# A recurrence's TensorE loop that covers all 64 blocks, entered at the first chunk and closed at the last

## The reference, cut to what matters

```python
def _step(Sm, inputs):
    q_t, k_t, v_t, beta_t = inputs
    Sk = jnp.einsum('bhde,bhe->bhd', Sm, k_t)
    delta = v_t - Sk
    Sm = Sm + beta_t[..., None] * jnp.einsum('bhd,bhe->bhde', delta, k_t)
    o_t = jnp.einsum('bhde,bhe->bhd', Sm, q_t)
    return (Sm, o_t)
...
outputs, then:  outputs @ wo + bo
```

## Time and profile before

| | us |
|---|---|
| median of 3 runs | 3170.09 (3166.7 to 3174.82) |
| the profiled execution's time | 3168.27 |
| its span in the trace | 3166.5 |
| TensorE busy | 3037.5 (96%) |
| VectorE busy | 1941.0 (61%) |
| ScalarE busy | 1420.6 (45%) |
| GpSimd busy | 1222.5 (39%) |
| chain that ended last, share of TensorE | 83% |

### The profile page before, as it was taken

The page is one execution under the profiler, slowest core; times in us unless marked ns, Lnnn a source line. Parts: engine busy times, 40 slices in busy tenths (PEclk is TensorE's granted clock), DMA queues, the critical chain, the costliest instruction groups (busy, mean ns, idle before and its releaser), DMA issues.

```text
span 3166.5 us, 148606 instructions
## 1 busy us (share of the span) xinstructions
PE 3037.5 (96%) x67876; PEld 2488.1 (79%) x67876; DVE 1941.0 (61%) x3190; ACT 1420.6 (45%) x3226; POOL 1222.5 (39%) x1225
## 2 busy tenths in 40 slices
PE   5999999999968999999999999999999999999998
PEld 4777777777757999999888787877778787777876
DVE  5888878878758999998513443444444344444434
ACT  5554545444413555555454433444443344444334
POOL 1446565655635877766311221112222112122211
PEclk8999999999978999999999999999999999999999
DMA  3545555554575777777661232222222222222220
GB/s 105 161 141 179 156 161 160 153 163 141 161 224 170 225 227 229 230 217 215 200 201 57 68 79 67 58 76 77 57 70 77 67 58 76 77 58 73 73 67 27
DMA packets 471354, 402.34 MB, mean 127 GB/s; under 512 B 68032, under 2 KB 391744, under 8 KB 471104
## 3 DMA queue, kind: packets, MB, share of 16 engines
q1 hardware_dynamic: 460960, 382.39, 41.5%
q10 hardware_dynamic: 10144, 16.63, 1.8%
HBM read 199.69 MB, written 153.09 MB: 111 GB/s over the span
## 4 chain that ended last, share of the span: by engine, by line
PE 83%; DVE 7%; issue 4%; SPq 3%; DMA 2%; ACT 1%; POOL 0%; DVEq 0%; ACTq 0%
PE bank L238 18%; PE bank L240 17%; PE bank L239 17%; PE bank L1280 14%; PE bank L1365 6%; SPq L1697 3%; PE bank L477 3%; PE bank L429 2%; DMA x2T<-HT 1%; PE bank L438 1%; PE bank L1769 1%; PE bank L421 1%; PE bank L1758 1%; PE bank L412 1%; DVE tmp L1527 1%
## 5 line engine op out<-in xcount | busy, mean ns | idle before, releaser
L2015 DVE TENSOR_TENSOR glo<-gl,gh 128x512 fp32r<-128x512 f32 x256 | 202.0, 789 | 702.5 <-ACT gh L1887 701.0
L1883 ACT ACTIVATE gl<-bank,b1m 128x512 f32<-128x512 f32 x256 | 176.3, 689 | 693.7 <-PE bank L240 693.7
L238 PE MATMUL bank<-h,w_hi 128*128 128x512 f32 x1024 | 404.8, 395 | 0.1
L240 PE MATMUL bank<-h,w_lo 128*128 128x512 f32 x1024 | 400.4, 391 | 0.0
L240 PE MATMUL bank<-w_hi,glo 128*128 128x512 f32 x1024 | 399.6, 390 | 0.0
L238 PE MATMUL bank<-w_hi,gh 128*128 128x512 f32 x1024 | 399.3, 390 | 0.0
L239 PE MATMUL bank<-h,w_hi 128*128 128x512 f32 x1024 | 398.8, 389 | 0.0
L239 PE MATMUL bank<-w_lo,gh 128*128 128x512 f32 x1024 | 398.3, 389 | 0.0
L1280 PE MATMUL bank<-ringA 32*32 32x32 f32 x16384 | 344.0, 197 | 12.9 <-issue 8.1
L1280 PEld LDWEIGHTS bank<-ringA 32*32 32x32 f32 x16384 | 271.7, 105 | 11.5 <-issue 6.0
L238 PEld LDWEIGHTS bank<-h,w_hi 128*128 128x128 f32 x1024 | 192.1, 188 | 67.6 <-issue 29.0
(11 more groups left out here) (195 smaller groups left out, 7284.2 us busy)
## 6 DMA issues: line engine op xcount, KB each, us to landing
ringB<-heads_scratch SPq DMA_DIRECT2D x256, 192.0 KB, 3.4
ringA<-heads_scratch SPq DMA_DIRECT2D x256, 128.0 KB, 2.6
x2T<-HT SPq DMA_DIRECT2D x480, 64.0 KB, 2.1
X<-in_L_attn_x SPq DMA_DIRECT2D x16, 1024.0 KB, 10.2
x_scratch<-X SPq DMA_DIRECT2D x16, 1024.0 KB, 4.2
heads_scratch<-vb SPq DMA_DIRECT2D x16, 1024.0 KB, 6.1
heads_scratch<-qk SPq DMA_DIRECT2D x16, 1024.0 KB, 7.2
heads_scratch<-kb SPq DMA_DIRECT2D x16, 1024.0 KB, 5.2
```

Of the source, the lines that this page charges most:

```text
L238: e.matmul(o, lhs[0], rhs[0], start=first, stop=False)
L240: return e.matmul(o, lhs[1], rhs[0], start=False, stop=last)
L1883: e.activation(ordered, made, ACT.Gelu_apprx_tanh, bias=b1m[:, m:m + 1]).then_inc(a_gl, 1)
L2015: e.tensor_tensor(gh[k][1][:, :], gl[k][:, :], gh[k][0][:, :], ALU.subtract).then_inc(v_gl, 1)
```

## The change

The loop now runs 64 times over chunks 0, 1, the product, 2, 3. Ahead of it stand only `keys(0)` and the two `values(0)`. Behind it come the transposes and the last product. So the loop closes after a chunk's small matmuls instead of after the product. As the body always prepares the next chunk, the SP queue loads a 257th chunk (with the last one's data) that is prepared and not used. The first pass has a product of block -1: `oT_hi` and `oT_lo` are now cleared in full ahead of it, and every wait on `p_wo` counts one more. The clearing decrements of `a_delta` and `d_B` move from the next chunk's `deltas` into `states`.

```diff
-            deltas(0)
             e.wait_ge(d_B[0], 16)
-            states(0)
-            emptied(deltas(1), 0)
-            states(1)
-            e.wait_ge(v_olo[1], 1)
-
-            with nc.Fori(0, NBLK - 1, 1, engines=bass.OrderedEngineSet([mybir.EngineType.PE]),
+            with nc.Fori(0, NBLK, 1, engines=bass.OrderedEngineSet([mybir.EngineType.PE]),
                          hint_back_edge=True, head_slot={mybir.EngineType.PE: 0}):
+                deltas(0)
+                e.wait_ge(v_olo[0], 1)
+                states(0)
+                deltas(1)
+                states(1)
+                e.wait_ge(v_olo[1], 1)
+                out_product(range(12))
                 made = deltas(2)
-                emptied(made, 1)
                 made[4].then_inc(v_olo[0], -1)
                 made[5].then_inc(v_olo[1], -1)
                 states(2)
-                emptied(deltas(3), 2)
+                deltas(3)
                 states(3)
-                emptied(deltas(0), 3)
-                e.wait_ge(v_olo[0], 1)
-                states(0)
-                emptied(deltas(1), 0)
-                states(1)
-                e.wait_ge(v_olo[1], 1)
-                out_product(range(12))
-            emptied(deltas(2), 1)
-            states(2)
-            emptied(deltas(3, last=True), 2)
-            states(3, last=True)
...
-            e.wait_ge(v_olo[0], 2)
-            e.wait_ge(v_olo[1], 2)
+            e.wait_ge(v_olo[0], 1)
+            e.wait_ge(v_olo[1], 1)
             out_product(range(12))
...
                 made[1].then_inc(a_state[j], -2)
+                made[2].then_inc(a_delta[j], -2)
+                made[3].then_inc(d_B[j], -16)
...
-                if q >= 2:
-                    e.wait_ge(p_wo, q // 2)
+                e.wait_ge(p_wo, q // 2 + 1)
...
-            e.memset(oh[0][:, :, 0:1].bitcast(F32), 0.0).then_inc(v_olo[0], 1)
-            e.memset(oh[1][:, :, 0:1].bitcast(F32), 0.0).then_inc(v_olo[1], 1)
+            e.memset(oh[0][:, :, :].bitcast(F32), 0.0).then_inc(v_olo[0], 1)
             for k in range(NF):
...
             m.then_inc(v_z, 16)
+            e.memset(oh[1][:, :, :].bitcast(F32), 0.0).then_inc(v_olo[1], 1)
...
-                if c + 4 < CHUNKS:
+                if c + 4 <= CHUNKS:
```

More of the change, by code:

```diff
@@ L250, in load_a @@
             def load_a(c):
-                s = c // NC
+                n = min(c, CHUNKS - 1)
+                s = n // NC
                 if c >= 4:
                     e.wait_ge(p_delta, 2 * (c - 4) + 1)
-                if s and c % NC == 0:
+                if s and n % NC == 0:
                     e.wait_ge(v_back, 4 * s)
-                e.dma_start(ringA[:, c % 4, RK:RV + 1, :], heads_d[c, :, K2:V2 + 1, :]).then_inc(d_A[c % 4], 16)
+                e.dma_start(ringA[:, c % 4, RK:RV + 1, :], heads_d[n, :, K2:V2 + 1, :]).then_inc(d_A[c % 4], 16)
                 if s:
                     e.dma_start(ringA[:, c % 4, RX, :],
-                                xt[s % 2][:, c % NC, :, :].rearrange("p n i -> p (n i)")).then_inc(d_A[c % 4], 16)
+                                xt[s % 2][:, n % NC, :, :].rearrange("p n i -> p (n i)")).then_inc(d_A[c % 4], 16)
                 else:
                     e.dma_start(ringA[:, c % 4, RX, :],
-                                xt_d[c].rearrange("p n i -> p (n i)")).then_inc(d_A[c % 4], 16)
+                                xt_d[n].rearrange("p n i -> p (n i)")).then_inc(d_A[c % 4], 16)
             def load_b(c):
@@ L267, in load_b @@
                     e.wait_ge(p_o, c - 3)
-                e.dma_start(ringB[:, c % 4, :, :], heads_d[c, :, Q2:B2 + 1, :]).then_inc(d_B[c % 4], 16)
+                e.dma_start(ringB[:, c % 4, :, :], heads_d[min(c, CHUNKS - 1), :, Q2:B2 + 1, :]).then_inc(d_B[c % 4], 16)
             return load_system, load_a, load_b
@@ L1324, in out_delta, with deltas @@
                              False)
-            def deltas(j, last=False):
+            def deltas(j):
                 e.wait_ge(a_state[j], 1)
@@ L1330, in deltas @@
                 made[1].then_inc(d_A[j], -32)
-                if not last:
-                    e.wait_ge(d_A[(j + 1) % 4], 32)
-                    keys((j + 1) % 4)
+                e.wait_ge(d_A[(j + 1) % 4], 32)
+                keys((j + 1) % 4)
                 e.wait_ge(a_state[j], 2)
@@ L1336, in deltas, with states @@
                 return made
[L1338 to L1343, removed]
+            def states(j):
                 after = (j + 1) % 4
@@ L1348, in states @@
                 state(j, FRONT)
-                if not last:
-                    values(after, FRONT)
-                    e.wait_ge(d_B[after], 16)
+                values(after, FRONT)
+                e.wait_ge(d_B[after], 16)
                 out_delta(j, FRONT)
@@ L1354, in states @@
                 state(j, BACK)
-                if not last:
-                    values(after, BACK)
+                values(after, BACK)
                 made = out_delta(j, BACK)
                 made[1].then_inc(a_state[j], -2)
+                made[2].then_inc(a_delta[j], -2)
+                made[3].then_inc(d_B[j], -16)
                 made[-1].then_inc(p_o, 1)
@@ L1547, in add_out @@
                 i = blk % 2
-                e.wait_ge(p_wo, blk + 1)
+                e.wait_ge(p_wo, blk + 2)
                 e.wait_ge(o_yb, blk + 1)
                 e.tensor_tensor(zb[i][:, :], bank[B_WO][:, :], zb[i][:, :], ALU.add).then_inc(v_z, 8)
-            e.memset(oh[0][:, :, 0:1].bitcast(F32), 0.0).then_inc(v_olo[0], 1)
-            e.memset(oh[1][:, :, 0:1].bitcast(F32), 0.0).then_inc(v_olo[1], 1)
+            e.memset(oh[0][:, :, :].bitcast(F32), 0.0).then_inc(v_olo[0], 1)
             for k in range(NF):
```

## The result

The changed kernel takes 3178.64 us (median of 8 runs, 3173.5 to 3183.48) against 3167.97 us before (8 runs); the ratio is 1.0035, 95% interval [1.0025, 1.0045]. It is slower by 0.35%, about 11 us. The forecast was 19.5 us slower. The direction and the mechanism held, the time lies just inside the low end of the range (3178 to 3200), and the largest term was nearly twice too large.

The account below looks back on a forecast made before the run. TensorE, without slack in the recurrence, was taken as the bound, with code loading and VectorE at the start. Branch +24.9, start -3.5, end -1.9 gave +19.5 us on 3168.3, with 1.8 for the median 3189.6 us; range 3178 to 3200.

Parts of the forecast that it names:

- The closing branch: Between chunk 3 and chunk 0, once a pass: add, branch and hint stop matmul issue for 0.43 us, bounds 0 to 0.57.
- 58 at 0.43 us: +24.9 us: Branch taken 63 times; the first counted in the start, four hidden in waits for VectorE, the other 58 exposed.
- I take the whole 0.43 us as exposed: At the end of chunk 3 the queue of small matmuls is near empty, so it covers none of the pause.
- Nothing: Parts taken to cost nothing: three extra ring loads, the clearing decrements, the changed counts of `p_wo`.
- The start: Loop entry and first pass: two chunks removed, a product of zeros added; block 0's product ends 4 to 7 us sooner.
- I take -3.5 us: Net gain at the start, after VectorE sets the pace from `low(2)` to 1030 us; bounds -1 and -8 us.
- The end: Chunks 254 and 255 run in the loop instead of loading written-out code: -1.9 us, bounds 0 and -2.5.
- The range: Pause of 0.28 to 0.57 us and gains of 2 to 9 us: +8 to +30 us, 3178 to 3200 us.
- The branch hides: Rival, chance 0.13: queued weight loads shrink the pause to 0.08 us or nothing; 3165 to 3169 us.
- The loop's head is fetched anew: Rival, chance 0.03: each taken branch fetches its target, at least 2.19 us a pass, 138 us in all, near 3310 us.
- The clock falls: Rival, chance 0.02: the pause drops the granted clock in each pass, 2 us and more a pass, over 100 us.
- the gap's releaser: Sign: TensorE idle about 0.4 us once a pass between chunk 3 and chunk 0, with releaser "issue".

Follow-up runs that it names:

- pause8_product: Kernel before with eight always-satisfied waits right behind the product's last matmul, ahead of the add and branch; median pass 10.79 us.
- before_no_hint: Kernel before without the prefetch hint of the loop's closing branch; 3168.75 us, ratio 0.999, median pass 10.79 us.
- pause runs: Kernel before with four or eight always-satisfied waits between chunk 3 and chunk 0, no branch there; median passes 10.87 and 11.11 us.
- clear_early: Kernel before with only the clearing decrements of a_delta and d_B moved from deltas into states; 3166.28 us, ratio 0.9994.
- after_old_clearing: Changed kernel with the clearing decrements of a_delta and d_B put back in the next chunk's deltas; 3186.7 us, ratio 1.0058.
- the spread pair: Kernel before and changed kernel, each with the first system's solver steps over 27 chunks instead of 24; 3172.63 and 3180.03 us.
- after_no_hint: Changed kernel without the prefetch hint of the closing branch; 3171.35 us, ratio 1.0008, median pass 10.93 us.

## Why the prediction was right, and where its largest term was off

*The closing branch.* Right in place, cause and length: a gap of 0.40 us once a pass where 0.43 was forecast, nothing while a product lies over it (pause8_product, before_no_hint), no code loading and no fallen clock. Mis-sized was the term "58 at 0.43 us: +24.9 us", by the step "I take the whole 0.43 us as exposed". It measured +13.1 us over 57 passes. Of these 1.7 us come from one pass, that of block 53, where TensorE waits for a `ringA` transfer (17.0 us before, 19.0 after); it need not be the loop's, since that pass takes 17.0 to 19.6 us in the ten profiles with the old loop. The rest is 0.20 us a pass in that mean, 0.22 in the median. The account of a pass from the runs:

| | us |
|---|---|
| gap 0.40 less the 0.01 of before | +0.39 |
| first 32 records behind the gap, faster behind any pause (pause runs) | -0.06 |
| clearing of chunk 1 under the product (clear_early) | -0.06 |
| clearing of chunk 3 under the gap (after_old_clearing less the line above) | -0.06 |
| sum | +0.21 |
| measured | +0.22 |

For the first of these I had a hint in hand: the earlier trace rows show small matmuls running faster behind a product, and I read them only as a sign that the queue is empty at the branch. The other two I had struck out under "Nothing", where the prediction lists "the clearing decrements". That step failed: a decrement isn't free because nobody waits for it.

The pass itself was 0.05 us too long, 10.84 us for 10.79: the window 1060 to 1542 ends inside a product, which has few records for its time, so records over 780 count too few passes.

*The start.* Right up to `low(2)`: TensorE led by 4.2 us at the product of block 0, forecast 4 to 7. Too large was "I take -3.5 us" at block 5, where 1.2 are left. From `low(2)` VectorE sets the pace, as forecast, but its work up to there took 8.9 us where the window of the earlier trace rows had 8.0, so `low(2)` had 2.6 us of lead and not 4; and the lead shrinks by 1.2 us more up to `low(4)`. That the load on VectorE is what eats it is shown by the spread pair. Why its same work took longer is not.

*The end.* -1.9 us forecast up to the transposes, -1.9 measured, with the stop of 2.19 us gone. The 1.5 us that the transposes and the last product gain at full clock were not in the sum.

*The range.* That it held is in part luck. Its low end, +8 us, was made of a pause of 0.28 us and gains of 9 us at the ends (58 x 0.28 - 9 is +7). The pause was 0.40 us and the gains 1.2 and 1.9 us, or 4.6 with the clock; what brought the time down there was what comes back behind the gap, of which the sum had nothing.

*The rivals.* "The branch hides" falls: the gap is there in full. "The loop's head is fetched anew" falls by after_no_hint. "The clock falls": the granted clock is 1.00 over 1060 to 1540 us. Of the signs named, the gap's releaser was wrong (ScalarE in the page's words, not "issue"), and the passes are 11.0 and not 11.2 to 11.3 us.

*Open.* The stretch from the end of the last product to the end of the program takes 1498.1 us in the profile before and 1503.4 after, 5.2 us more, mostly waits for the `x2T` transfers (1.8 us before, 5.6 after). No instruction there changed. With the stage ahead, 3.3 us shorter in the second execution, the parts of the difference are -3.3, +9.9, -1.5 and +5.2, together the 10.4 us between the two executions. The other nine profiles with the old loop have 1497.7 to 1501.2 us, the other three with the changed loop 1500.9 to 1502.9; the means are 3 us apart. So some 3 of the measured 11 us may come from behind the recurrence, and neither the forecast nor any run here explains them.

## What to carry to other kernels

Put a hardware loop's closing branch where the engine still has long work queued: here twelve large matmuls hid it, and behind small matmuls it opened a gap of 0.4 us in each pass. Before taking written-out ends into a loop, set what their code loading costs once (here 1.9 us at the end and 1.5 more by the clock, 1.2 left at the start) against what the new place of the branch costs each time. Then look at who paces the stretch where the gain falls: an engine that is late anyway takes the gain, and a quicker TensorE finds it late again.

## What the hardware showed that I had not expected

A clearing decrement on a matmul costs the stream about 26 ns (0.05 to 0.06 us for a pair), some 35 small-matmul records after the matmul that carries it, and nothing if a product or a pause lies there. Five such decrements brought under the product took the median pass from 10.79 to 10.64 us. Why they cost is not shown; the runs show only how much, where, and that it moves with them. Whether an increment on a matmul costs the same was not tried.

The prefetch hint costs 0.08 us a pass where the branch is exposed (11.01 and 10.93 us), and the loop of six code blocks didn't need it.

The profile names as releaser whoever updated a semaphore last, although the wait had been over: a gap of the sequencer behind small matmuls read as a wait for `sT`.
